# Attention on one core: the maxima's products, and the last scores, issued twice in a row

## The chip, the core and the metric

The kernel runs on one core of a Trainium2 chip. Its time is the device time in microseconds (us); three runs of the kernel before gave 4300.12, 4308.26 and 4286.41, with a median of 4300.12. A core has TensorE (PE, matrix products into the banks of PSUM; its weight loads are shown apart as PEld), VectorE (DVE), ScalarE (ACT), GpSimd (POOL) and SyncE (SP, which issues the transfers). TensorE's clock is granted by the chip: the profile shows it as 1.00 (2.4 GHz) or 0.50 (1.2 GHz), or as a mean of both over a longer stretch.

## What is computed

Two layers follow one another on an input of 2 batches of 1024 tokens of 512 values: attention with 32 heads of 16 values, a gated feed-forward block with low-rank factors, a state-space block ("mamba"), and a second feed-forward block. Each stands between two layer norms and is added to its input. The change touches the attention alone:

```python
q = (x @ Wq.T + bq).reshape(b, l, h, hd).transpose(0, 2, 1, 3)
k = (x @ Wk.T + bk).reshape(b, l, h, hd).transpose(0, 2, 1, 3)
v = (x @ Wv.T + bv).reshape(b, l, h, hd).transpose(0, 2, 1, 3)
scores = jnp.einsum('bhqd,bhkd->bhqk', q, k) / math.sqrt(hd)
scores = jnp.where(causal, scores, -jnp.inf)
att = jax.nn.softmax(scores, axis=-1)
out = jnp.einsum('bhqk,bhkd->bhqd', att, v)
```

## The kernel before

**Tiling.** The batches run one after the other. In a batch the attention goes through eight "quads" of four heads (t = 0 to 7). Queries and keys are split into a high and a low part, and three products of 16 values each stand stacked as one product over 48 rows (`stack_q`, `stack_k`). The scores are wanted twice. First with the queries as rows, 48 products of 48 rows in a quad ("pieces", line 628): VectorE takes the maximum of each row of each product (lines 1237 and 1242), and nothing else is kept of them. The maxima are turned (line 637), split and put by two small transfers into two more rows of `stack_q`. Then the scores with the keys as rows, 48 products of 50 rows in a quad (line 652), which have the maxima subtracted already: ScalarE takes the exponential of two heads at once (line 948) into `probs`, GpSimd zeroes what lies above the diagonal (line 1608), and the products with V (line 671, four heads side by side in the array, each as two instructions) add up in bank 6. These outputs are copied, turned (line 681) and divided into Y.

**Sizes.** Of the twelve pieces of a head six have 512 columns and two each 384, 256 and 128, which is 384 in the mean; the twelve score products of a head have the same sizes.

**Order.** `attention_order()` writes out one order, `ORDER`, that all engines follow. Before quad 0's scores come the first projections, V and quad 0's pieces, with six pieces of quad 1. From then on quad t's scores are mixed with quad t+1's pieces: in each of the twelve steps of a quad four score products, each with a piece or two behind it, then the product with V of the step before. In quads 1 and 3 four projections are mixed in as well (48 products of 128 rows and 512 columns, lines 492 to 494). Quad 7 has no pieces beside it.

**Waits.** The pieces, projections and turns go round three banks (4, 5, 7). A piece waits for `ring_free`, which says that VectorE has read the bank three places before; it raises `ring_done`, for which VectorE waits. The scores use banks 0 to 3: the first of each pair waits for `exp_done` of the step before, the second raises `st_done`, for which ScalarE waits.

Of the kernel before, what the change touches and what calls it, by code (L numbers as in the profile page):

```python
# [24 lines left out]
P = 128  # L25
TT = L // P
KT = D // P
HALF = 512
# [6 lines left out]
NQ = AH // QUAD  # L35
VW = HD + 1
ROWS = 3 * HD
# [26 lines left out]
def build(nc, x, w_attn, qk_bias, bv, bo, w_ffn0, lr0, lr0_const, w_ffn1,  # L64
          w_mamba, w_dt, conv_par, dt_bias, a_log, d_skip, out):
    ctx = ExitStack()
    with ctx:
        def sb(name, shape, dt=F32, stack=ctx):
            return stack.enter_context(nc.sbuf_tensor(name, shape, dt))
# [5 lines left out]
        bank = [banks[:, i, :] for i in range(8)]  # L75
# [26 lines left out]
        with ExitStack() as s:  # L102
            V = sb("V", [P, TT, AH, VW], stack=s)
            with ExitStack() as s2:
                stack_q = [sb("stack_q0", [P, QUAD, L], F32R, stack=s2)]
                stack_k = [sb("stack_k0", [P, QUAD, L], F32R, stack=s2)]
# [380 lines left out]
        def _(pe):  # L487
            pe.wait_ge(consts_ready, 1)

            def three(dst, a_hi, a_lo, w_hi, w_lo, kt, first, last):  # L490

                pe.matmul(dst, a_hi(kt), w_hi(kt), start=first, stop=False)  # L492
                pe.matmul(dst, a_lo(kt), w_hi(kt), start=False, stop=False)  # L493
                return pe.matmul(dst, a_hi(kt), w_lo(kt), start=False, stop=last)  # L494

            def tokens(dst, i, w_hi, w_lo, cols=None):

                tok = slice(i * P, (i + 1) * P)
                for kt in range(KT):
                    r = three(dst, lambda k: xhi[:, k, tok], lambda k: xlo[:, k, tok],  # L500
                              lambda k: w_hi[:, k, :], lambda k: w_lo[:, k, :], kt, kt == 0, kt == KT - 1)
                return r

            def features(dst, w_hi, w_lo, s):

                tok = slice(s * HALF, (s + 1) * HALF)
                for kt in range(KT):
                    r = three(dst, lambda k: w_hi[:, k * P:(k + 1) * P], lambda k: w_lo[:, k * P:(k + 1) * P],
                              lambda k: xhi[:, k, tok], lambda k: xlo[:, k, tok], kt, kt == 0, kt == KT - 1)
                return r  # L510
# [85 lines left out]
            with pe.Fori(0, B) as b:  # L596
# [5 lines left out]
                for what, *arg in ORDER:  # L602
                    if what == "proj":
                        f, use = arg
                        which = use // 2
                        if use == 0:
                            pe.wait_ge(wqk_ready, b * 8 + 2 * f + 2)
                        if ring >= 3:
                            pe.wait_ge(ring_free, b * RING + ring - 2)
                        features(bank[RING_BANKS[ring % 3]][:], wqk_hi[:, which, :], wqk_lo[:, which, :], use % 2  # L610
                                 ).then_inc(ring_done, 1)
                        ring += 1
                    elif what == "values_in":
                        i, = arg
                        if i == 0:
                            pe.wait_ge(wv_ready, b + 1)
                        pe.wait_ge(ring_free, b * RING + ring - 2)
                        tokens(bank[RING_BANKS[ring % 3]][:], i, wv_hi, wv_lo).then_inc(ring_done, 1)
                        ring += 1
                    elif what == "piece":  # L620
                        t, n = arg
                        h, i, s, cols, _ = PIECES[n]
                        base, buf = 64 * (t % 2), t // 2 % 2
                        if n == 0:
                            pe.wait_ge(stacked[t % 2], (b * (NQ // 2) + t // 2 + 1) * STACKED)
                        pe.wait_ge(ring_free, b * RING + ring - 2)
                        dst = bank[RING_BANKS[ring % 3]]
                        r = pe.matmul(dst[:, 0:cols], stack_q[buf][base:base + ROWS, h, i * P:(i + 1) * P],  # L628
                                      stack_k[buf][base:base + ROWS, h, s * HALF:s * HALF + cols],
                                      start=True, stop=True)  # L630
                        r.then_inc(ring_done, 1)
                        ring += 1
                    elif what == "maxima":
                        t, = arg
                        pe.wait_ge(mx_ready, b * NQ + t + 1)
                        pe.wait_ge(ring_free, b * RING + ring - 2)
                        pe.transpose(bank[RING_BANKS[ring % 3]][0:QUAD * TT, 0:P], mx[:, 0, :], ident[:]
                                     ).then_inc(ring_done, 1)
                        ring += 1
                    elif what == "score":  # L640
                        t, n, h = arg
                        s, j = STEPS[n]
                        lo = max(j * P - s * HALF, 0)
                        base, buf = 64 * (t % 2), t // 2 % 2
                        it = b * (NQ * NS) + (t * NS + n)
                        if n == 0 and h == 0 and t % 2 == 0 and t < 4:
                            pe.wait_ge(ones_rows, b * (16 * 8) + 16 * 4 * (t // 2 + 1))
                        if n == 0 and h == 0:
                            pe.wait_ge(mt_in, START + (b * NQ + t + 1) * 32)
                        if h % 2 == 0:  # L650
                            pe.wait_ge(exp_done[h // 2], START + it)
                        r = pe.matmul(bank[h][:, 0:HALF - lo],  # L652
                                      stack_k[buf][base:base + ROWS + 2, h, j * P:(j + 1) * P],
                                      stack_q[buf][base:base + ROWS + 2, h, s * HALF + lo:(s + 1) * HALF],
                                      start=True, stop=True)
                        if h % 2:
                            r.then_inc(st_done[h // 2], 1)
                    elif what == "values":
                        t, n = arg
                        s, j = STEPS[n]  # L660
                        lo = max(j * P - s * HALF, 0)
                        it = b * (NQ * NS) + (t * NS + n)
                        if j == 0:
                            pe.wait_ge(ot_ready, START + b * (2 * NQ) + 2 * t + s)
                        for p in range(2):
                            if j * P >= s * HALF:
                                pe.wait_ge(masked[p], b * (NQ * TT) + (t * TT + j + 1))
                            else:
                                pe.wait_ge(exp_done[p], START + it + 1)
                        for h in range(QUAD):  # L670
                            r = pe.matmul(bank[6][32 * h:32 * h + VW, lo:HALF], V[:, j, QUAD * t + h, :],  # L671
                                          probs[n % 2][:, h, 0:HALF - lo], start=j == 0,
                                          stop=j == CPH * (s + 1) - 1, skip_group_check=True,
                                          tile_position=(0, 32 * h))
                        r.then_inc(pv_done, 1)
                    elif what == "turn":
                        t, s = arg
                        pe.wait_ge(ot_ready, START + b * (2 * NQ) + 2 * t + s + 1)
                        pe.wait_ge(ring_free, b * RING + ring - 2)
                        for k in range(CPH):  # L680
                            r = pe.transpose(bank[RING_BANKS[ring % 3]][:, k * P:(k + 1) * P], ot[:, k * P:(k + 1) * P], ident[:])
                        r.then_inc(ring_done, 1)
                        ring += 1
# [3 lines left out]
                for i in range(TT + 1):  # L687
                    if i < TT:
                        if i >= 2:
                            pe.wait_ge(at_free, b * TT + i - 1)  # L690
                        for k in range(KT):
                            r = pe.transpose(bank[2 + i % 2][:, k * P:(k + 1) * P], Y[:, i, k * P:(k + 1) * P],
                                             ident[:])
# [17 lines left out]
                for s in range(2):  # L711
                    tok = slice(s * HALF, (s + 1) * HALF)
                    for kt in range(KT):
                        r = three(bank[5 + s][0:MH, :], lambda k: wdt_hi[:, k, :], lambda k: wdt_lo[:, k, :],
                                  lambda k: xhi[:, k, tok], lambda k: xlo[:, k, tok], kt, kt == 0, kt == KT - 1)
# [1072 lines left out]
```

## Time and profile before

| | |
|---|---|
| median of three runs | 4300.12 us |
| the profiled execution | 4294.83 us |
| its span, first to last instruction | 4293.1 us |
| mean granted clock of TensorE | 0.907 |
| attention of batch 0 (29 to 478 us) | 449 us at a clock of 0.76 |
| attention of batch 1 (2178 to 2640 us) | 462 us at 0.77 |
| PE busy, share of the span | 90% |

The profile lists what each engine did and when. PE's busy time counts a product from its start to its modelled end, so products that overlap in the pipeline make it look fuller than its columns would. The distance from one start to the next in a dense stream is what a product costs.

### The profile page before, as it was taken

To read this page: it belongs to the slowest core of one execution; us is meant where nothing else is said; L and a number is where in the kernel's file an instruction comes from. 1 tells how busy PE (TensorE), PEld (TensorE's weight loads), DVE (VectorE), ACT (ScalarE), POOL (GpSimd) and SP (SyncE) were. 2 spreads that over 40 slices of the span, in tenths; PEclk is the share of its full clock that TensorE was granted. 3 is DMA by queue.
4 is the path that set the end of the run, shared out by engine and by line. 5 is a ranking of instruction groups with operands and counts; after the bars stand their busy time and mean duration, and the time that the engine had idled before them with its cause. 6 is when DMAs were issued, how large, how long until landed. Compare 5 with 4: busy or idle time off the path is not lost.

```text
span 4293.1 us, 61464 instructions
## 1 busy us (share of the span) xinstructions
PE 3861.4 (90%) x18056; PEld 2813.5 (66%) x18056; DVE 2711.2 (63%) x5034; ACT 1695.2 (39%) x3538; POOL 1880.8 (44%) x2017
## 2 busy tenths in 40 slices
PE   7899799689999999979878896996899999999797
PEld 4444478567777777757654444885677777777576
DVE  3567445577777777764435673555777777777644
ACT  1344411355545555541113444113555555555411
POOL 1111344355555655654311113443555556655542
PEclk8677899899999999989977767998999999999899
DMA  3221011011100111001032210110101001110010
GB/s 73 36 36 31 24 51 45 22 33 30 32 20 25 34 32 29 22 15 45 35 81 36 36 32 29 46 45 22 35 28 32 20 25 34 32 29 22 15 52 35
DMA packets 81456, 145.59 MB, mean 34 GB/s; under 512 B 16392, under 2 KB 18520, under 8 KB 81264
## 3 DMA queue, kind: packets, MB, share of 16 engines
q1 hardware_dynamic: 81264, 143.28, 12.9%
q8 instruction: 90, 1.47, 0.1%
q14 instruction: 102, 0.84, 0.1%
HBM read 113.08 MB, written 4.19 MB: 27 GB/s over the span
## 4 chain that ended last, share of the span: by engine, by line
PE 69%; issue 11%; DVE 7%; ACT 4%; POOL 3%; DVEq 2%; POOLq 2%; DMA 1%; SPq 1%; ACTq 0%
PE banks L492 15%; PE banks L493 14%; PE banks L494 14%; PE banks L832 4%; PE banks L671 4%; PE banks L652 3%; PE banks L628 3%; PE banks L825 2%; PE banks L845 2%; DVE conv L1344 2%; DVEq L1347 1%; PE banks L767 1%; PE banks L768 1%; POOL X L1509 1%; ACT conv L1005 1%
## 5 line engine op out<-in xcount | busy, mean ns | idle before, releaser
L1344 DVE SCALAR_TENSOR_TENSOR conv<-banks,cpar,conv 128x509 f32<-128x509 f32 (+2 forms) x576 | 428.2, 744 | 115.3 <-ACT conv L1005 100.9
L948 ACT ACTIVATE probs<-banks 128x1024 f32<-128x1024 f32 (+3 forms) x384 | 297.7, 810 | 309.4 <-PE banks L652 308.9
L1172 DVE TENSOR_TENSOR Y<-banks,Y 128x512 f32<-128x512 f32 x400 | 276.1, 691 | 188.1 <-PE banks L494 187.9
L1608 POOL TENSOR_SCALAR_AFFINE_SELECT probs<-probs 128x256 f32<-128x256 f32 x256 | 104.2, 408 | 645.8 <-ACT probs L948 645.5
L628 PE MATMUL banks<-stack_k,stack_q 48*128 48x512 f32 (+3 forms) x768 | 331.7, 502 | 59.3 <-DVEq L1218 19.8
L1672 POOL TENSOR_TENSOR state<-state,gt 128x512 f32<-128x512 f32 x112 | 133.5, 1192 | 500.4 <-PE banks L825 500.4
L492 PE MATMUL banks<-xhi,f_hi 128*128 128x512 f32 x800 | 322.6, 403 | 3.5 <-DVE xlo L1143 3.5
L492 PE MATMUL banks<-xhi,wx_hi 128*128 128x512 f32 x768 | 312.0, 406 | 14.4 <-DVE conv L1344 14.4
L493 PE MATMUL banks<-xhi,f_lo 128*128 128x512 f32 x800 | 319.9, 400 | 0.0
L494 PE MATMUL banks<-xlo,f_hi 128*128 128x512 f32 x800 | 319.4, 399 | 0.0
L494 PE MATMUL banks<-xlo,wx_hi 128*128 128x512 f32 x768 | 306.0, 398 | 0.0
L493 PE MATMUL banks<-xhi,wx_lo 128*128 128x512 f32 x768 | 306.0, 398 | 0.0
L1237 DVE CUSTOM_DVE_ANT_0 banks<-banks,mask_qk 128x128 f32<-128x128 f32 (+3 forms) x512 | 248.1, 500 | 72.7 <-PE banks L628 59.4
L832 PEld LDWEIGHTS banks<-xdt,decay 128*128 128x128 f32 x2048 | 248.5, 192 | 65.2 <-issue 65.2
L652 PE MATMUL banks<-stack_q,stack_k 50*128 50x512 f32 (+3 forms) x768 | 274.7, 459 | 5.2 <-ACT probs L948 2.9
L628 PEld LDWEIGHTS banks<-stack_k,stack_q 48*128 48x128 f32 x768 | 163.0, 235 | 157.9 <-DVE mx L1242 51.1
L492 PE MATMUL banks<-wg_hi,xhi 128*128 128x512 f32 x512 | 222.3, 434 | 45.5 <-DVE conv L1344 42.2
L652 PEld LDWEIGHTS banks<-stack_q,stack_k 50*128 50x128 f32 x768 | 157.0, 232 | 155.5 <-issue 116.8
L832 PE MATMUL banks<-xdt,decay 128*128 128x64 f32 x2048 | 242.7, 272 | 2.4 <-DVE decay L1363 2.4
L910 ACT CAST h_hi<-hf 128x512 fp32r<-128x512 f32 x100 | 62.2, 622 | 441.0 <-DVE hf L1161 441.0
L518 PE MATMUL banks<-ident,xn 128*128 128x128 f32 x256 | 66.5, 426 | 188.1 <-ACT xn L892 165.3
L1076 ACT ACTIVATE yv<-banks,gt 128x64 f32<-128x64 f32 x1024 | 223.8, 332 | 24.8 <-PE banks L825 24.8
(209 smaller groups left out, 10185.0 us busy)
## 6 DMA issues: line engine op xcount, KB each, us to landing
m_raw<-in_w_mamba SPq DMA_DIRECT2D x224, 256.0 KB, 2.6
f_raw<-in_w_ffn SPq DMA_DIRECT2D x50, 768.0 KB, 4.5
stack_q<-part_hi SPq DMA_DIRECT2D x128, 64.0 KB, 2.4
stack_k<-part_hi SPq DMA_DIRECT2D x128, 64.0 KB, 2.5
X<-in_x SPq DMA_DIRECT2D x4, 1024.0 KB, 6.5
wqk_raw<-in_w_attn SPq DMA_DIRECT2D x8, 512.0 KB, 3.5
stack_q<-part_lo SPq DMA_DIRECT2D x64, 64.0 KB, 2.4
stack_k<-part_lo SPq DMA_DIRECT2D x64, 64.0 KB, 2.5
```

Source lines behind the costliest of these rows:

```text
L492: pe.matmul(dst, a_hi(kt), w_hi(kt), start=first, stop=False)
L493: pe.matmul(dst, a_lo(kt), w_hi(kt), start=False, stop=False)
L494: return pe.matmul(dst, a_hi(kt), w_lo(kt), start=False, stop=last)
L628: r = pe.matmul(dst[:, 0:cols], stack_q[buf][base:base + ROWS, h, i * P:(i + 1) * P], stack_k[buf][base:base + ROWS, h, s * HALF:s * HALF ...
L652: r = pe.matmul(bank[h][:, 0:HALF - lo], stack_k[buf][base:base + ROWS + 2, h, j * P:(j + 1) * P], stack_q[buf][base:base + ROWS + 2, h, s ...
L671: r = pe.matmul(bank[6][32 * h:32 * h + VW, lo:HALF], V[:, j, QUAD * t + h, :], probs[n % 2][:, h, 0:HALF - lo], start=j == 0, stop=j == C ...
L832: r = pe.matmul(bank[7][:, h * MP:(h + 1) * MP], decay[:, h, :], xdt[:, h * MP:(h + 1) * MP], start=True, stop=True, skip_group_check=True)
L948: act.activation(probs[n % 2][:, 2 * p:2 * p + 2, 0:w], banks[:, 2 * p:2 * p + 2, 0:w], ACT.Exp, scale=1.0 / HD ** 0.5).then_inc(exp_done[ ...
L1076: r = act.activation(yv[:, own], bank[6][:, own], ACT.Identity, scale=gt[:, EC, c, h:h + 1])
L1172: dve.tensor_tensor(Y[:, i, :], bank[6 + i % 2], Y[:, i, :], ALU.add).then_inc(f["dn_used"], 1)
L1237: dve.tensor_tensor_reduce(out=src, in0=src, in1=mask_qk[:, HALF - cols:HALF], scale=1.0, scalar=NEG, op0=ALU.add, op1=ALU.max, accum_out= ...
L1344: r = dve.scalar_tensor_tensor(out=rest, in0=src[:, 0:HALF - lag], scalar=cpar[:, o:o + 1], in1=rest, op0=ALU.mult, op1=ALU.add)
```

## The change

The product for the maxima is issued once for quad 0 and twice for quads 1 to 7, both times with the same operands into the same columns of the same bank; the waits stand ahead of the first, and `ring_done` is raised by the second. The score products of quad 7 are issued twice in the same way, and `st_done` is raised by the second of the pair's second head. All results stay the same, and no other engine's program changes. Each product loads its weights itself, so a weight load is added with each.

```diff
@@ piece
                         dst = bank[RING_BANKS[ring % 3]]
-                        r = pe.matmul(dst[:, 0:cols], stack_q[buf][base:base + ROWS, h, i * P:(i + 1) * P],
-                                      stack_k[buf][base:base + ROWS, h, s * HALF:s * HALF + cols],
-                                      start=True, stop=True)
+                        for _ in range(1 if t == 0 else 2):
+                            r = pe.matmul(dst[:, 0:cols], stack_q[buf][base:base + ROWS, h, i * P:(i + 1) * P],
+                                          stack_k[buf][base:base + ROWS, h, s * HALF:s * HALF + cols],
+                                          start=True, stop=True)
                         r.then_inc(ring_done, 1)
@@ score
                             pe.wait_ge(exp_done[h // 2], START + it)
-                        r = pe.matmul(bank[h][:, 0:HALF - lo],
-                                      stack_k[buf][base:base + ROWS + 2, h, j * P:(j + 1) * P],
-                                      stack_q[buf][base:base + ROWS + 2, h, s * HALF + lo:(s + 1) * HALF],
-                                      start=True, stop=True)
+                        for _ in range(2 if t == NQ - 1 else 1):
+                            r = pe.matmul(bank[h][:, 0:HALF - lo],
+                                          stack_k[buf][base:base + ROWS + 2, h, j * P:(j + 1) * P],
+                                          stack_q[buf][base:base + ROWS + 2, h, s * HALF + lo:(s + 1) * HALF],
+                                          start=True, stop=True)
                         if h % 2:
                             r.then_inc(st_done[h // 2], 1)
```

## Rows read from the trace of the kernel before

**Rows 1.** The page's slices: busy tenths of PE, and the granted clock.
```profile
PE   7899799689999999979878896996899999999797
PEclk8677899899999999989977767998999999999899
```
**Rows 2.** Busy time by stretch: both attentions, their parts with pieces, their last quads.
```profile
core 0: us, PE busy (x) PEld busy (x) DVE busy (x) ACT busy (x) POOL busy (x), PEclk, DMA share, GB/s
29.00:478.00 449.00, 406.23 (x1903) 206.18 (x1904) 245.40 (x738) 159.67 (x209) 70.35 (x137) 0.76 0.20 36
2178.00:2640.00 462.00, 418.67 (x1981) 218.38 (x1981) 253.01 (x748) 163.78 (x215) 68.73 (x136) 0.77 0.20 35
...
123.00:446.00 323.00, 300.72 (x1488) 140.82 (x1492) 204.69 (x631) 135.69 (x176) 51.64 (x114) 0.72 0.20 34
2272.00:2590.00 318.00, 294.71 (x1500) 138.16 (x1499) 203.14 (x623) 137.78 (x178) 52.80 (x117) 0.74 0.22 37
```
**Rows 3.** The stretches at low clock between 123 and 437 us, all instructions: thirteen stretches.
```profile
123.00:157.50 34.50, 33.40 (x135) 15.40 (x137) 22.42 (x73) 13.28 (x16) 3.27 (x8) 0.50 0.61 103
...
369.10:396.40 27.30, 27.19 (x117) 11.38 (x115) 16.86 (x54) 10.54 (x14) 2.45 (x6) 0.50 0.00 1
410.10:437.40 27.30, 27.23 (x118) 11.61 (x117) 17.11 (x54) 10.95 (x14) 2.74 (x7) 0.50 0.00 1
sum 181.20, PE 177.15 PEld 80.43 DVE 104.67 ACT 62.34 POOL 21.67; mean PE 13.63 PEld 6.19 DVE 8.05 ACT 4.80 POOL 1.67
```
**Rows 4.** The stretches at high clock between 157 and 446 us: thirteen stretches.
```profile
352.00:369.10 17.10, 16.00 (x110) 7.61 (x106) 13.64 (x44) 9.97 (x13) 4.08 (x10) 1.00 0.25 43
396.40:410.10 13.70, 12.60 (x86) 6.12 (x86) 11.40 (x36) 7.64 (x11) 3.80 (x10) 1.00 0.02 5
...
sum 141.80, PE 123.58 PEld 60.39 DVE 100.03 ACT 73.35 POOL 29.97; mean PE 9.51 PEld 4.65 DVE 7.69 ACT 5.64 POOL 2.31
```
**Rows 5.** Batch 1's twelve stretches at low clock, 2270 to 2574 us: all instructions, their sum.
```profile
sum 167.10, PE 163.31 PEld 75.03 DVE 100.46 ACT 56.33 POOL 23.48; mean PE 13.61 PEld 6.25 DVE 8.37 ACT 4.69 POOL 1.96
```
**Rows 6.** Line 628 alone in the low-clock stretches of batch 0 (170 in all).
```profile
123.00:157.50 34.50, 20.75 (x41) 10.88 (x42) 0.50 0.61 103
...
369.10:396.40 27.30, 14.25 (x28) 7.05 (x27) 0.50 0.00 1
410.10:437.40 27.30, 14.59 (x28) 7.29 (x28) 0.50 0.00 1
```
**Rows 7.** The same in the low-clock stretches of batch 1 (159 in all).
```profile
2270.30:2297.60 27.30, 17.55 (x34) 8.86 (x33) 0.50 0.63 106
...
2546.80:2574.10 27.30, 16.02 (x31) 8.02 (x31) 0.50 0.01 2
```
**Rows 8.** Timeline at low clock (start, length): products of 512 columns in a dense stream.
```profile
178.10 0.63 PE L492 MATMUL banks<-xhi,wqk_hi 128*128 128x512 f32 x1
178.53 0.63 PE L493 MATMUL banks<-xhi,wqk_lo 128*128 128x512 f32 x1
178.95 0.63 PE L494 MATMUL banks<-xlo,wqk_hi 128*128 128x512 f32 x1
```
**Rows 9.** Stretches of 20 us in the attention and in the feed-forward block.
```profile
240.00:260.00 20.00, 20.00 (x91) 9.36 (x93) 13.05 (x41) 9.07 (x11) 0.50 (x2) 0.50 0.61 99
...
2700.00:2720.00 20.00, 20.00 (x91) 16.30 (x91) 9.63 (x14) 3.04 (x5) 11.98 (x13) 1.00 0.13 41
```
**Rows 10.** The page on line 628: all of both batches, and what PE's idle time before it waited for.
```profile
L628 PE MATMUL banks<-stack_k,stack_q 48*128 48x512 f32 (+3 forms) x768 | 331.7, 502 | 59.3 <-DVEq L1218 19.8
```
**Rows 11.** Line 628 from 123 to 446 us: PE's idle time before it, by releaser.
```profile
L628 PE MATMUL banks<-stack_k,stack_q x336: 217/496/794, 123.5 to 441.7; 48*128 48x512 f32 x112, 48*128 48x128 f32 x28, 48*128 48x384 f32 x28
its engine sat idle before it (us, times) until:
  DVE mx L1242: 27.4, 71
  DVE mx L1237: 18.9, 45
  DVEq L1218: 16.0, 16
```
**Rows 12.** The last 3.4 us at high clock ahead of a fall, and the last quad.
```profile
454.40:478.00 23.60, 20.28 (x143) 8.91 (x143) 3.17 (x7) 14.75 (x21) 11.28 (x14) 1.00 0.00 1
...
365.70:369.10 3.40, 3.12 (x19) 1.70 (x15) 3.22 (x10) 2.62 (x3) 0.82 (x2) 1.00 0.01 2
```
**Rows 13.** Groups of instructions from 446 to 478 us, quad 7 of batch 0.
```profile
L948 ACT ACTIVATE probs<-banks 128x1024 f32<-128x1024 f32 (+3 forms) x25 | 18.5, 792 | 9.1 <-PE banks L652 9.1
L652 PE MATMUL banks<-stack_q,stack_k 50*128 50x512 f32 (+3 forms) x48 | 13.1, 381 | 1.7 <-ACT probs L948 1.5 <-DMA stack_q<-mt_lo 0.2
```
**Rows 14.** The timeline from 365.7 to 368.2 us on PE and ACT, ahead of the same fall.
```profile
365.73 0.49 PE L652 MATMUL banks<-stack_q,stack_k 50*128 50x512 f32 x1
...
365.73 0.50 PE L628 MATMUL banks<-stack_k,stack_q 48*128 48x512 f32 x1
...
367.56 0.44 PE L652 MATMUL banks<-stack_q,stack_k 50*128 50x384 f32 x1
...
368.14 0.50 PE L628 MATMUL banks<-stack_k,stack_q 48*128 48x512 f32 x1
```

## The prediction

> **What bounds the kernel now.** I read the page's slices first: PE is busy nearly everywhere, but the granted clock is below 1.00 mostly in the slices of the two attentions [rows 1]. Then busy time by stretch: the attentions last 449 and 462 us with a mean clock of 0.76 and 0.77, while VectorE is busy 245 of the 449 and ScalarE 160 [rows 2]. So TensorE sets the pace, at a clock that changes. I therefore cut the part in which pieces and scores are mixed (123 to 446 us, and 2272 to 2590) at every change of the clock, and asked for each kind of stretch by itself. At low clock PE is busy 177 of 181 us in batch 0 and 163 of 167 in batch 1 [rows 3, 5]: whatever is added there is paid in full. At high clock it is busy 124 of 142 us and VectorE 100 [rows 4]; a typical one, 396.4 to 410.1, has VectorE at 11.4 of 13.7. There the two engines run close together, and PE waits for VectorE to free a bank: before line 628 it sat idle 27.4 and 18.9 us for the two kinds of maximum and 16.0 us for the drain behind a projection, out of 323 us [rows 11]. The reader is to see that the mixed part has two regimes of about equal work, one with no slack on PE and one with some.
>
> **How many, and at what price.** The change adds products and their weight loads on TensorE, moves nothing, removes nothing, and touches no queue and no transfer. Pieces of quads 1 to 7: 7 x 48 x 2 batches = 672 of 48 rows. Scores of quad 7: 48 x 2 = 96 of 50 rows. A product of 512 columns costs 0.427 us at low clock, from start to start in a dense stream [rows 8], and 20.00 / 92 = 0.217 us at high clock (91 to 92 in 20 us, [rows 9]). The mean piece has 384 columns, three quarters of it: 0.320 and 0.163 us. The rows of price are of 128-row products; for 48 rows there is no dense stream in the trace to read it from, but 117 and 118 products fill 27.3 us at low clock wholly [rows 3], so I take the same price and no surcharge. The weight load lies beside the product ahead of it: it is busy 11.4 of the 27.3 us in which the products are busy all the time [rows 3]. For the smallest pieces (128 columns, two of twelve) the load might not be hidden; even at 0.1 us for each of those 112, an estimate as large as half the 0.213 us that 256 columns take at low clock, it would be 11 us, and I leave it to the range.
>
> **The pieces at low clock.** Of line 628's products 170 lie in low-clock stretches in batch 0 and 159 in batch 1 [rows 6, 7]; a second issue of each costs 329 x 0.320 = 105 us. PE's idle time there is 4 + 4 us in all, so I count it whole: +105. What it delays is everything behind it in PE's queue: the next score, for which ScalarE waits, and the next product with V. VectorE, which waits for `ring_done`, starts each maximum 0.32 us later, with 105 of 181 us busy it has room.
>
> **The pieces at high clock.** The other 672 - 329 = 343 cost 343 x 0.163 = 56 us of PE. Here PE has slack, but it isn't free for them: the second issue stands behind the same wait as the first, so it can hide only by running while the other two banks of the ring still hold work for VectorE. Bounds: 0 (all in the gaps) and 56 (all on the path). In the stretch 396.4 to 410.1 PE is busy 12.6 of 13.7 us, whose 21 pieces would add 3.4 us; VectorE needs 11.4. Neither covers it all. I take half, +28.
>
> **The scores of quad 7.** 96 x 0.163 = 15.6 us. ScalarE is busy 18.5 of 32 us there and idle 9.1 us waiting for these very products [rows 13]; each pair's exponential starts two products later than before. Bounds 0 and 16; PE is not full (20.3 of 23.6 us, [rows 12]) but most of the chain goes through it. I take two thirds, +10.
>
> **The clock.** The sum so far holds the clock of each stretch as it was. What does the doubled work do to it? The trace shows when it falls. From 365.7 to 369.1 PE is busy 3.12 of 3.40 us, almost only with products of 48 and 50 rows [rows 12, 14], and behind it the clock is 0.50 for 27.3 us [rows 3]. Quad 7 has no pieces, PE is emptier (20.28 of 23.60), and it keeps 1.00 all through [rows 12]. And 240 to 260 us has PE busy 20.00 of 20.00 at 0.50 the whole time, where the feed-forward block with as full a PE runs at 1.00 [rows 9]. So products of 48 rows, even dense, have not held the clock in this kernel; the products over 128 rows (V, projections) do. Doubling the pieces makes the mix poorer in those. I take no gain and no loss of clock for the forecast.
>
> The Trainium skill ("TensorE: Matmul & The Clock Gate", Part 1, and its table of goals) says that the clock follows how busy the PE has been, and advises to keep it busy without gaps; by that the filler products would raise it. The rows on 240 to 260 us and 365.7 to 369.1 us disagree with busy time alone as the measure; what that rule would give here is rival A.
>
> **Sum.** 105 + 28 + 10 = +143 us on the profiled execution's 4294.8 us: 4438 us. The profiled execution lies 5 us under the median of the runs shown, so against the median it is +3.2%.
>
> **Rivals.**
>
> A, the clock stays up (faster). The second issue fills the gaps of the high-clock stretches, above all at the border of two quads where the clock falls now, and the low stretches vanish. Price: the 181 + 167 = 348 us at low clock would be bounded by VectorE, busy 104.7 + 100.5 = 205 us there [rows 3, 5]; in a high stretch it is 11.4 of 13.7, or 0.83, so they would last 205 / 0.83 = 247 us, 101 less. All 672 pieces are then issued at 0.163, 110 us, of which half on the path, 55, and quad 7's 10: -36, so 4259 us. It decides at the border of quads: if the clock is still 1.00 there, nothing later pulls it down. For it: the gap to a full PE is small there, and the trace has no stretch of 48-row products without any gap at high clock. Against it: PE was already busy 3.12 of 3.40 and the clock fell.
>
> B, part of it. Some of the falls are avoided, those that come where products with V stand among the pieces, others not. Halfway between the forecast and A: 4349 us.
>
> C, the clock falls more. The high stretches end earlier since 128-row products lie further apart. A high stretch does 86 products in 13.7 us and a low one 117 in 27.3 [rows 3, 4], 6.3 against 4.3 per us, so each us of high clock that turns low costs 0.47 us. If a quarter of the 142 + 154 us at high clock turns, that is 74 x 0.47 = 35 us and some 10 us more because the added pieces there lose their cover: 4438 + 45 = 4483 us.
>
> D, hidden or without effect: the second issue costs nothing since another wait ends last. It would need slack where PE is busy 177 of 181 us; about 4300 to 4320.
>
> **Chances.** Forecast 0.50, A 0.13, B 0.17, C 0.14, D 0.06. About 0.5% (21 us) is what a measurement of this kernel can tell from no change. Faster by over 0.5%: A, 0.13. Within 0.5%: most of D and the lower edge of B, 0.08. Slower: the rest, 0.79. The forecast's own bounds are 105 + 0 + 0 and 105 + 56 + 16 + 11, so 4400 to 4483. For 8 in 10 I reach up to C (4495) and down through most of B (4330), which leaves out A, D and the far end of C.
>
> **What would show it.** Right: 768 more products on PE, line 628 with 1440 instead of 768 [rows 10]; the mixed parts some 65 us longer each, with a mean clock near the 0.72 and 0.74 of before; low-clock stretches of a quad without projections some 36 instead of 27 us; quad 7 about 5 us longer; all else unchanged. Wrong: a clock of 1.00 across the border of quads, with VectorE at over 0.8 of the mixed part (A); high stretches shorter than 13.7 us in quads 5 and 6 (C). If pieces at high clock turn out wholly hidden, 28 us go; if a score in quad 7 is hidden too, 10 more.

## The result, and the profile after

The changed kernel took 4346.44 us (median of four runs, 4335.71 to 4355.68) against 4299.14 for the kernel before on the same chip: a ratio of 1.010, 95% interval 1.008 to 1.013. It is slower, as forecast, but by 47 us and not by 143. The profiled execution has a span of 4353.9 us, 60.8 more than the one before; it is the slowest of the four runs, 9 us above their median.

The page of the changed kernel: the two slices of [rows 1], the counts of [rows 10], and ScalarE's group. Its lines below 628 have moved down by one or two: 629 are the pieces, 654 the scores, 673 the products with V.

```profile
PE   7999889789999999979779998897899999999797
PEclk8797889899999999989977987898999999999899
...
L629 PE MATMUL banks<-stack_k,stack_q 48*128 48x512 f32 (+3 forms) x1440 | 432.4, 431 | 46.3 <-DVEq L1220 17.4
L950 ACT ACTIVATE probs<-banks 128x1024 f32<-128x1024 f32 (+3 forms) x384 | 303.4, 810 | 359.6 <-PE banks L654 358.8
```

The 1440 pieces are there, 672 more. What answers to [rows 2] is the busy time of the same two stretches and of both attentions (start and end, length, then busy us of PE, PEld, DVE, ACT and POOL, the granted clock, and DMA):

```profile
29.00:503.00 474.00, 439.73 (x2281) 259.37 (x2282) 252.84 (x737) 162.50 (x208) 70.16 (x137) 0.80 0.20 34
2200.00:2678.00 478.00, 443.37 (x2282) 257.63 (x2283) 250.62 (x737) 162.80 (x208) 69.72 (x137) 0.79 0.19 34
...
123.00:446.00 323.00, 305.78 (x1725) 174.39 (x1724) 205.19 (x612) 129.00 (x164) 49.02 (x108) 0.79 0.21 34
2272.00:2590.00 318.00, 296.24 (x1626) 168.33 (x1625) 196.35 (x585) 121.13 (x154) 45.00 (x99) 0.81 0.21 35
```

The part in which pieces and scores are mixed runs at a *higher* clock than before, 0.79 and 0.81 for 0.72 and 0.74. That is against the forecast. What happened is seen quad by quad. I took the turn of the maxima (one small transpose on PE for each quad) as the border of the quads. First the kernel before, quads 2, 5 and 6 of batch 0:

```profile
224.30:265.60 41.30, 39.75 (x202) 18.09 (x201) 28.60 (x89) 18.59 (x25) 6.53 (x16) 0.67 0.54 91
361.20:402.60 41.40, 40.14 (x201) 17.55 (x201) 28.55 (x89) 18.62 (x25) 6.53 (x16) 0.67 0.01 2
402.60:443.70 41.10, 39.89 (x201) 17.73 (x201) 28.51 (x89) 18.61 (x25) 6.53 (x16) 0.67 0.01 2
```

and its quad 7 in both batches:

```profile
443.70:477.20 33.50, 28.28 (x187) 12.02 (x188) 4.68 (x11) 19.82 (x28) 14.50 (x22) 0.95 0.12 41
...
2583.60:2617.50 33.90, 28.80 (x188) 12.48 (x188) 4.68 (x11) 19.78 (x28) 14.49 (x22) 0.91 0.13 41
```

Then the changed kernel: quads 2, 5, 6 and 7 of batch 0, and 2, 4, 5, 6 and 7 of batch 1:

```profile
234.40:270.50 36.10, 34.93 (x251) 18.57 (x250) 28.67 (x89) 18.75 (x24) 6.50 (x16) 1.00 0.62 102
...
366.70:414.50 47.80, 47.44 (x250) 27.57 (x250) 30.42 (x89) 19.11 (x24) 6.50 (x16) 0.64 0.01 2
414.50:462.40 47.90, 47.55 (x251) 27.79 (x250) 30.53 (x89) 19.12 (x24) 6.51 (x16) 0.64 0.01 2
462.40:502.80 40.40, 37.08 (x236) 20.91 (x236) 4.68 (x11) 20.46 (x28) 14.56 (x22) 0.90 0.11 34
...
2405.70:2441.80 36.10, 34.94 (x250) 18.59 (x250) 28.66 (x89) 18.76 (x25) 6.50 (x16) 1.00 0.60 101
...
2501.60:2537.40 35.80, 34.64 (x250) 18.44 (x249) 28.46 (x89) 18.72 (x25) 6.50 (x16) 1.00 0.55 90
2537.40:2586.80 49.40, 49.05 (x250) 27.92 (x249) 30.47 (x89) 19.12 (x25) 6.51 (x16) 0.62 0.01 2
2586.80:2622.60 35.80, 34.64 (x250) 18.45 (x249) 28.48 (x89) 18.73 (x25) 6.50 (x16) 1.00 0.01 3
2622.60:2677.70 55.10, 52.21 (x236) 27.68 (x236) 4.68 (x11) 21.07 (x28) 14.52 (x22) 0.61 0.07 25
```

The reader is to see two kinds of quad in the place of one among quads 2 and 4 to 6, which have no projections. Before, each was a mixture, 38 to 41 us at a clock of 0.67 to 0.78. After, four of the eight are wholly at high clock and *shorter* than before, 36 us, with 48 more products in them (a fifth, quad 4 of batch 0, nearly so: 37.2 us at 0.95), and in three the clock fell for long and they take 48 to 49. Quad 7 went from 33.5 and 33.9 to 40.4 and 55.1 us. Added up, quads 0 to 6 of both batches cost 24 us more in these two traces (half of it in quad 0), quad 7 costs 28, and the part ahead of quad 0, which the change doesn't touch, 7 (98.1 and 98.0 us against 94.1 and 94.7, at a clock of 0.79 and 0.76 against 0.84 and 0.81).

### The profile page after: what moved, and what is told of

Its sections match the earlier page's. It is cut to its first block, busy times and chain, and to the rows that moved or that the text cites. A ratio compares the mean times of both kernels' runs of the same rounds, so it can differ in the third digit from the quotient of the medians.

```text
span 4353.9 us, 63000 instructions
## 1 busy us (share of the span) xinstructions
PE 3940.6 (91%) x18824; PEld 2922.9 (67%) x18824; DVE 2724.1 (63%) x5034; ACT 1699.9 (39%) x3538; POOL 1878.1 (43%) x2017
## 4 chain that ended last, share of the span: by engine, by line
PE 71%; issue 11%; DVE 6%; ACT 4%; POOL 3%; POOLq 2%; DVEq 2%; SPq 1%; DMA 1%; ACTq 0%
PE banks L492 15%; PE banks L493 14%; PE banks L494 14%; PE banks L629 6%; PE banks L834 4%; PE banks L673 4%; PE banks L654 4%; PE banks L827 2%; PE banks L847 2%; DVE conv L1346 2%; DVEq L1349 1%; PE banks L769 1%; PE banks L770 1%; POOL X L1511 1%; ACT conv L1007 1%
## 5 line engine op out<-in xcount | busy, mean ns | idle before, releaser
L629 PE MATMUL banks<-stack_k,stack_q 48*128 48x512 f32 (+3 forms) x1440 | 432.4, 431 | 46.3 <-DVEq L1220 17.4
L629 PEld LDWEIGHTS banks<-stack_k,stack_q 48*128 48x128 f32 x1440 | 276.2, 227 | 134.9 <-DVE mx L1244 40.5
L654 PE MATMUL banks<-stack_q,stack_k 50*128 50x512 f32 (+3 forms) x864 | 290.4, 441 | 0.4 <-DMA stack_q<-mt_lo 0.4
L654 PEld LDWEIGHTS banks<-stack_q,stack_k 50*128 50x128 f32 x864 | 171.2, 222 | 131.3 <-issue 114.0
```

The source lines that it names most:

```text
L654: r = pe.matmul(bank[h][:, 0:HALF - lo], stack_k[buf][base:base + ROWS + 2, h, j * P:(j + 1) * P], stack_q[buf][base:base + ROWS + 2, h, s ...
```

## The experiments

Each run's median is set against the kernel before on the same chip, with the ratio and its 95% interval in brackets. The medians of before are 4301.38 us for the first four runs, 4310.65 for the next four and 4301.29 for the last four. The theories: **R**, the clock follows how much of the array's rows the products fill, so fillers (added products whose results nobody uses) over more rows hold it better; **B**, PE's busy time alone sets it; **pure cost**, the prediction's sum with no effect on the clock.

**One part alone: the pieces twice, quad 7's scores once.**

```diff
-                        for _ in range(2 if t == NQ - 1 else 1):
-                            r = pe.matmul(bank[h][:, 0:HALF - lo],
+                        r = pe.matmul(bank[h][:, 0:HALF - lo],
```

> The products for the maxima twice, the scores of quad 7 once. In the changed kernel quad 7 took 40.4 us in batch 0 and 55.1 in batch 1, against 33.5 and 33.9 before, so 28 of its 59 us more in the span came from the doubled scores. Theory R (the clock follows how much of the array's rows the products fill; doubled 48-row products hold it if it is high and can't bring it back if it is low): the rest remains, 4346 - 28 = 4318 us, with some quads near 36 us wholly at high clock and some near 48 us mostly at low clock. Theory B (busy time alone sets the clock): the same time, 4318, so it is the fillers below that part R and B. Rival C of pure cost (the prediction's sum, no effect on the clock): 4300 + 133 = 4433 us.

Measured: 4342.28 us (ratio 1.008, 1.005 to 1.011; ten runs from 4313.9 to 4351.9, the last of them the traced one). Pure cost, 4433, is out, and so is the 4318 of R and B: the 28 us of quad 7 did not come back. Quad 6 and quad 7 of batch 0:

```profile
422.10:458.10 36.00, 34.84 (x251) 18.58 (x250) 28.60 (x90) 18.74 (x24) 6.52 (x16) 1.00 0.01 3
458.10:504.10 46.00, 42.48 (x189) 17.61 (x188) 4.68 (x11) 20.32 (x28) 14.51 (x22) 0.56 0.08 30
```

Quad 7 has nothing added, has a quad wholly at high clock ahead of it, and yet runs at 0.56 and takes 46 us, where it took 33.5 in the kernel before. So the time of quad 7 changes with what came before, even in code that is unchanged. The clock goes down in it in the kernel before as well, at nearly the same place, but comes back. The stretches at low clock of quad 7 of batch 0, in the kernel before and in this run:

```profile
451.00:454.40 3.40, 3.35 (x15) 1.29 (x15) 0.26 (x1) 0.92 (x2) 0.82 (x2) 0.50 0.18 67
```

```profile
463.60:504.10 40.50, 38.10 (x152) 15.59 (x153) 3.43 (x8) 17.79 (x24) 12.92 (x18) 0.50 0.06 23
```

They begin 7.3 and 5.5 us after the quad does. It is the return of the clock that differs.

**The other part alone: quad 7's scores twice, all else as before.**

```diff
+                        for _ in range(2 if t == NQ - 1 else 1):
+                            r = pe.matmul(bank[h][:, 0:HALF - lo],
```

> The scores of quad 7 twice, everything else as before. Pure cost: 2 x 5 us, 4310. Theory R: quad 7 has only 50-row products and those with V, doubling the first thins out the second, so a quad that falls to low clock can't leave it: between +13 us (both batches at high clock, 40 us each) and +43 us (both at low clock, 55 us each), 4313 to 4343. Theory B: fuller PE holds the clock, +13 at the most.

Measured: 4355.94 us (1.012, 1.007 to 1.017), more than the whole change and outside what I expected. Quad 7 was at low clock in both batches:

```profile
443.00:496.30 53.30, 49.79 (x236) 27.15 (x235) 4.68 (x11) 20.55 (x28) 14.50 (x22) 0.66 0.08 26
2623.00:2683.30 60.30, 57.05 (x237) 30.30 (x236) 4.72 (x12) 21.19 (x28) 14.49 (x22) 0.56 0.07 23
```

That is 20 and 26 us more than before for 48 products each. PE was fuller than before in both (93% and 95%, after 84% and 85%), so busy time alone (B) doesn't hold the clock. Quads 0 to 6 of batch 1, where nothing was added, took 329 us in this trace and 315 in that of before: single traces differ by such amounts in unchanged code.

**Fillers over 128 and over 16 rows.** The first of the two products is replaced by another one of as many columns, whose result the second writes over.

```diff
+                        if t > 0:
+                            pe.matmul(dst[:, 0:cols], xhi[:, h, i * P:(i + 1) * P], xhi[:, h, 0:cols],
+                                      start=True, stop=True)
                         r = pe.matmul(dst[:, 0:cols], stack_q[buf][base:base + ROWS, h, i * P:(i + 1) * P],
```

> As the maxima twice, but the first of the two is a product of the same columns over 128 rows (of the normed input, thrown away: the second one writes over it). Same number of products and columns as in the run with the maxima twice. Theory R: the clock stays at 1.00 in quads 0 to 6, each of the quads without projections takes some 36 us as those at high clock did in the changed kernel (41 before), quads 1 and 3 some 56 (58 to 61 before): 8 x 4.5 + 2 x 4 + 4 x 3 = 56 us less than before, some 4245 us. Theory B: no different from the 48-row filler, 4318. Pure cost: 4433.

The filler of 16 rows takes rows `base` to `base + HD` of `stack_q` and `stack_k`.

> As the maxima twice, but the first of the two is a product over 16 rows alone, same columns, thrown away. Theory R: the clock is low in nearly all of quads 0, 2, 4, 5, 6, which take 48 to 50 us (41 before), and quads 1 and 3 some 65: 10 x 8 + 4 x 5 = 100 us more than before, some 4400 us. Theory B: as with the 48-row filler, 4318.

Measured: 4817.59 us and 4903.95 us (1.120 and 1.140). Neither theory had that, and R's forecast for 128 rows, 4245, failed by the most: the clock stayed down with the widest filler of all, with PE busy throughout. 80 us of the first run:

```profile
305.00:385.00 80.00, 80.00 (x230) 31.45 (x230) 27.97 (x78) 15.91 (x21) 5.28 (x13) 0.50 0.14 24
```

A filler's rows alone don't hold the clock, then. Both runs have a cost of their own, which makes them poor tests of it. The timeline of the first, PE alone, at low clock (start, length):

```profile
300.30 0.79 PE L629 MATMUL banks<-xhi 128*128 128x512 f32 x1
301.02 0.79 PE L631 MATMUL banks<-stack_k,stack_q 48*128 48x512 f32 x1
301.02 0.68 PE L655 MATMUL banks<-stack_q,stack_k 50*128 50x384 f32 x1
301.74 0.79 PE L629 MATMUL banks<-xhi 128*128 128x512 f32 x1
302.47 0.79 PE L631 MATMUL banks<-stack_k,stack_q 48*128 48x512 f32 x1
```

Between products of 128 rows and of 48 the starts are 0.72 us apart, where they are 0.427 in a stream of one kind [rows 8]: 0.29 us at each change. The Trainium skill ("TensorEngine Tiling (Array Packing)", Key Properties) says that changing the tiling mode drains the engine; the starts 0.29 us further apart agree with that. The timeline also shows something else: the piece (line 631) and the score product (655) start at the same time, 301.02. By their operands' partitions (`base = 64 * (t % 2)`, with t one apart) one stands in the lower 64 rows of the array and the other in the upper 64.

**Fillers over 64 and over 34 rows**, both in the same half of the rows as the piece, so that nothing is switched. Same number of products and columns, both from `xhi`; only the rows differ.

```diff
+                        if t > 0:
+                            pe.matmul(dst[:, 0:cols], xhi[base:base + 64, h, i * P:(i + 1) * P],
+                                      xhi[base:base + 64, h, 0:cols], start=True, stop=True)
```

> Each product for the maxima of quads 1 to 7 is preceded by one of the same columns over 64 rows of the normed input, in the same half of the array's rows (the fillers of 128 and of 16 rows changed the number of rows the array is set up for, and PE stood still at each change: this one doesn't). Its result is written over by the second. Theory R (what counts for the clock is the share of the array that works): more quads than with 48 rows twice stay at high clock from end to end (36 us), at least 9 of the 14 mixed ones: 4250 to 4300 us. Theory B (busy time alone): no different from the maxima twice, 4342 us.

> The same with a filler over 34 rows in the same half. Theory R: fewer quads at high clock throughout than with 48 rows twice (there 5 of the 8 without projections and past quad 0), at most 2: 4370 to 4420 us. Theory B: 4342 us as with the maxima twice.

Measured: 4297.74 us with 64 rows (0.998, 0.996 to 1.000) and 4429.58 with 34 (1.026, 1.022 to 1.031); with 48, above, 4342.28. The mean clock of the traced runs goes the same way, 0.924, 0.886 and 0.910. Three sizes, in order, 132 us from end to end with the same number of products and columns, and the runs of the three don't overlap: B is out, and R holds for fillers that leave the array's setting as it is. Its counts were off all the same. With 64 rows seven quads of the traced run are at 1.00 from end to end, where it asked for nine; with 48 there are six, with 34 none, and 4430 us lies above its 4370 to 4420. The 48-row fillers repeat the piece's own operands and ran on another chip, so the strict comparison is 64 against 34 rows. More rows also mean more values of `xhi` in the array; whether the data count beside the rows was not tested. With 64 rows, quads 5, 6 and 7 of batch 0 and quad 3 of batch 1:

```profile
365.90:403.80 37.90, 36.62 (x251) 19.25 (x250) 28.68 (x89) 18.81 (x24) 6.54 (x16) 0.95 0.01 2
403.80:439.70 35.90, 34.74 (x251) 18.56 (x250) 28.48 (x89) 18.75 (x24) 6.54 (x16) 1.00 0.01 3
439.70:485.10 45.40, 41.52 (x189) 17.20 (x188) 4.68 (x11) 20.22 (x28) 14.52 (x22) 0.58 0.09 30
2418.30:2473.40 55.10, 47.95 (x299) 27.20 (x298) 31.55 (x93) 21.83 (x28) 9.90 (x18) 1.00 0.03 6
```

With 34 rows, quads 5 and 6 of batch 0:

```profile
389.80:437.60 47.80, 47.45 (x250) 27.52 (x249) 30.36 (x89) 19.11 (x24) 6.50 (x16) 0.64 0.01 2
437.60:485.50 47.90, 47.55 (x250) 27.61 (x249) 30.51 (x89) 19.13 (x24) 6.50 (x16) 0.64 0.01 2
```

A quad at 1.00 takes 36 us with fillers of 64 as of 48 rows, and one at 0.64 takes 48 with 34 as with 48 rows: the rows change how long the clock is down, and not the price of the filler.

**Where the fillers must stand: the first 14 of a quad's 48, or the other 34.**

```diff
+                        for _ in range(2 if t > 0 and n < 14 else 1):
```

> Only the first 14 of a quad's 48 products for the maxima are issued twice, those that come in the last two steps of the quad before and the first two of its own, where the clock falls in the kernel before. Theory G (the gain is made at the border of quads, the price is paid by all fillers in low-clock stretches): a high clock survives the border as often as with all twice, and a quad at low clock costs 14/48 of the surcharge, 2.5 instead of 8 us: below 4300, some 4275 us. Rival H (the filler must be everywhere, since the clock falls inside the quad as well): 14/48 of the prediction's price of 133 us without a gain, 4340 us.

The other run has `n >= 14`.

> The complement: the other 34 of the 48 twice, none at the border. Theory G: the clock falls at the border as before, each of the 14 mixed quads has its low stretch, and 34/48 of the price is paid: 4300 + 94 = 4394 us, no quad of 36 us. Rival H: some quads stay high, about 4342 us.

Measured: 4321.98 us (1.002, 1.000 to 1.005) and 4351.19 (1.009, 1.006 to 1.012). Neither G nor H as I put them. With the border alone no quad was at 1.00 from end to end, though two came to 36.4 and 36.7 us; with the inside alone two took 36.3 us, with the clock down for 3.4 of them. So both places count. But these runs give the price of an added product at an unchanged mean clock. The border's fillers, quads 2 and 4, then the inside's, quad 5, all at 0.67:

```profile
226.40:268.30 41.90, 40.91 (x215) 20.23 (x215) 29.15 (x89) 18.74 (x25) 6.50 (x16) 0.67 0.52 90
329.20:371.00 41.80, 40.81 (x216) 20.24 (x216) 29.01 (x89) 18.74 (x25) 6.50 (x16) 0.67 0.48 77
```

```profile
367.00:413.00 46.00, 45.36 (x235) 24.30 (x234) 30.06 (x89) 18.75 (x24) 6.50 (x16) 0.67 0.01 2
```

The kernel before has 41.1 to 41.4 us at 0.67. The first 14 added products cost 0.5 us together, the other 34 cost 4.6 us: 0.04 and 0.14 us each.

**Fillers of 64 rows in quad 7 as well**, in all its twelve steps, or in the first four:

```diff
+                        if t == NQ - 1:
+                            pe.matmul(bank[h][:, 0:HALF - lo], xhi[base:base + 64, h, j * P:(j + 1) * P],
+                                      xhi[base:base + 64, h, s * HALF + lo:(s + 1) * HALF], start=True, stop=True)
```

> The fillers of 64 rows ahead of each product for the maxima of quads 1 to 7, as before in this study (4298 us), and one ahead of each of quad 7's 48 score products. Theory R: quad 7, which ran at low clock for 38 and 41 of its 45 and 46 us, keeps the high clock and takes 40 us, as the one with doubled scores at high clock did in the changed kernel: 2 x 5.5 us less, 4287. Theory B: PE is fuller, the same. If the fall comes from the wait for the transfers at the start of quad 7, where PE has nothing to do, fillers don't help and the quad takes 55 us: 4318.

> The same, but quad 7's fillers only in its first four steps of twelve, where the clock falls. Theory R: the quad keeps the high clock and then costs little more than the 33.5 us of the kernel before, some 35: 2 x 11 us less than 4298, 4276 us, below the kernel before (4300).

Measured: 4305.45 us (1.001, 0.999 to 1.003; twelve runs from 4278.4 to 4330.4) and 4302.60 (1.000, 0.998 to 1.002). With all twelve steps the traced run, 4283.4 us of span, has quad 7 as expected in both batches, where the clock goes down as before but comes back after 3.4 us. With the first four steps it fell all the same:

```profile
430.60:470.40 39.80, 36.38 (x237) 19.84 (x235) 4.68 (x11) 20.45 (x28) 14.56 (x22) 0.94 0.11 35
2571.00:2610.30 39.30, 35.80 (x235) 19.59 (x235) 4.68 (x11) 20.22 (x28) 14.56 (x22) 0.94 0.10 35
```

```profile
431.90:480.80 48.90, 45.81 (x206) 20.93 (x205) 4.70 (x12) 20.44 (x28) 14.53 (x22) 0.57 0.09 28
```

The forecasts of 4287 and 4276 us failed. The median of the first stays above its traced run by over 20 us; that quad 7 or others fall in many of its executions is likely, but a single trace can't say it.

**Fillers of 64 rows at the border and in quad 7's first four steps alone.**

```diff
-                        if t > 0:
+                        if t > 0 and n < 14:
```

> 64-row fillers only ahead of the first 14 products of each quad's 48 and in quad 7's first four steps. Theory R with the price at the fillers: the border holds the clock more often than with 48 rows there (4322), and the inside of a quad pays nothing: some 4270 us. If the inside needs them as well (the run with the inside alone twice kept two quads nearly all at high clock), it falls between: 4300.

Measured: 4313.41 us (1.002, 1.000 to 1.003), neither 4270 nor 4300. No gain; quads 2 and 4 to 6 come to 36.5 to 39.3 us at clocks below 1.00, but quad 7 takes 44.6 in both batches.

**The price by itself: the pieces three times.**

```diff
-                        for _ in range(1 if t == 0 else 2):
+                        for _ in range(1 if t == 0 else 3):
```

> Each product for the maxima three times, all over 48 rows. It measures the price of an added product by itself. If it is that of a stream of its own (the prediction's 0.320 us at low clock and 0.163 at high), a quad wholly at high clock goes from 36 to 44 us and one mostly at low clock from 49 to 64: 4342 + 14 x 11 = 4500 us. If an added product runs beside the score products in the other half of the rows, as the start times of the changed kernel suggest, half of it is hidden: 4342 + 14 x 5.5 = 4420 us.

Measured: 4456.38 us (1.035, 1.030 to 1.040), 114 us over two times, midway between the two prices. Quad 5 of batch 0, wholly at high clock, and quad 5 of batch 1, mostly at low:

```profile
401.20:442.50 41.30, 41.03 (x299) 26.32 (x298) 30.48 (x89) 19.25 (x24) 6.53 (x16) 1.00 0.01 3
...
2600.60:2659.10 58.50, 58.23 (x299) 36.05 (x298) 31.13 (x89) 19.47 (x24) 6.53 (x16) 0.67 0.01 2
```

At high clock the third product costs (41.3 - 36.0) / 48 = 0.11 us, and in a quad mostly at low clock (58.5 - 49.4) / 48 = 0.19 us, though at a mean clock of 0.67 where the quad with two had 0.62.

## Why the prediction was wrong in size

**What bounds the kernel: half right.** TensorE at a clock that changes, yes. "At low clock ... whatever is added there is paid in full" is the first step that failed. PE's modelled busy time, 177 of 181 us, was read as an array without slack. The array is two halves here: pieces of quad t+1 stand in one half of the rows and scores of quad t in the other, and they stream side by side. The trace of before shows it in the very rows that I quoted: at 365.73 us a score product and a piece start together [rows 14]. In the changed kernel at low clock (start, length; `x3` is three products in a row):

```profile
390.77 0.79 PE L654 MATMUL banks<-stack_q,stack_k 50*128 50x512 f32 x1
390.77 1.01 PE L629 MATMUL banks<-stack_k,stack_q 48*128 48x128 f32 x3
391.36 0.62 PE L654 MATMUL banks<-stack_q,stack_k 50*128 50x512 f32 x1
391.58 0.41 PE L629 MATMUL banks<-stack_k,stack_q 48*128 48x256 f32 x1
391.79 0.62 PE L654 MATMUL banks<-stack_q,stack_k 50*128 50x512 f32 x1
```

From the second on, the score products follow each other 0.43 us apart, the step of a dense stream at low clock, with the doubled small pieces wholly beside them. A second issue costs little as long as it runs beside a product of the other half; the third costs more, 0.11 us at high clock, with PE busy 41.0 of 41.3 us. The Trainium skill says that tiles of the array operate independently ("TensorEngine Tiling (Array Packing)", Key Properties), and the starts at 390.77 agree.

**The price: the low-clock term was mis-sized, by about three.** The terms were 0.320 us a piece at low clock (+105 us) and half of 0.163 at high (+28). At a clock of 0.67, 34 added products should have cost some 8 us, taking two thirds of them at low clock; they cost 4.6. For all 48, 14 + 34 together, that is 5.1 us a quad, so over 14 quads some 70 us where I had 133. This is worked out from quads without projections; that quads 1 and 3 pay the same was not measured.

The two kinds of quad give an estimate by another way. Before, a quad took 38.0 us with 17.1 at low clock (quad 4 of batch 0) and 41.1 with 27.3 (quad 6), so each us at low clock adds 0.30 and a quad wholly at high clock would take some 33. With 48 more it took 36.0 with none at low clock and 47.8 with 34.1, which is 0.35 for each. The 48 then cost some 3 us at high clock, or 0.07 each, close to the half of 0.163 that I took; and at the old 27.3 us of low clock some 4.4, of which 28 pieces at low clock pay some 3, or 0.11 each in the place of 0.320.

**The clock: the step that turned out wrong in kind.** "I take no gain and no loss of clock" and "products of 48 rows, even dense, have not held the clock". They do, when they are doubled: four quads of the traced run hold 1.00 from end to end, and six in the run with the pieces alone, in each of which it fell before. By the mean clocks of quads 0 to 6, 0.72 and 0.73 before, 0.79 and 0.83 after, the time at low clock went from some 350 to some 250 us. At 0.3 us each that is a gain of about 30 us, which with 14 x 4.4 = 62 us of price leaves some 30, near the 24 in the traces. The evidence that I drew on, 3.12 of 3.40 us busy ahead of the fall, was again modelled busy time.

The rival A was the right mechanism in the quads that hold (36 us, VectorE busy 28.7 of them, 0.79, near the 0.83 I used), and its point, the border of the quads, was one of two places. C, high stretches that end earlier, is not what happened in those that fell. Quads 5 and 6 of batch 0, in which the clock changes three times:

```profile
371.90:406.00 34.10, 34.10 (x155) 20.78 (x152) 20.38 (x57) 12.40 (x15) 3.25 (x8) 0.50 0.01 1
406.00:419.70 13.70, 13.35 (x100) 6.84 (x97) 10.05 (x32) 6.71 (x10) 3.25 (x8) 1.00 0.02 5
419.70:453.80 34.10, 34.10 (x159) 20.80 (x152) 20.47 (x57) 12.29 (x15) 3.26 (x8) 0.50 0.00 1
```

The high stretch is the 13.7 us of before, and the low ones are 34.1 for 27.3, close to the "some 36" of the forecast. So the forecast's picture came true in the three quads that fell and A's in those that hold. That is B, "part of it": 4349 us for 4346 measured. The number of B is partly luck, as it was a mere halfway value with quad 7 at +10; but that some quads would hold and others fall is what the trace shows.

**Quad 7: term mis-sized.** +10 us forecast, +28 in the trace, and +46 with its scores doubled alone. Mostly at high clock it costs 6.5 to 7 us a batch, not far from the 5 of the forecast (33.5 and 33.9 to 40.4). The rest is the fall: mostly at low clock it takes 55 us. I had said that quad 7 "keeps 1.00 all through". That was a wrong reading: the row from 454.4 to 478 us begins where the low stretch of 451.0 to 454.4, shown above, ends.

**The start of each attention**, 7 us in the trace, is in no part of the prediction. Its code is unchanged, and in batch 0 nothing that was changed has run before it. Among the traced runs it took 94.1 to 98.4 us in batch 0, so these 4 us at least are a difference between executions.

In the two traces, then, quads 0 to 6 cost 24 us where the sum had 133, quad 7 costs 28 where it had 10, and 7 lie ahead of them where it had nothing.

**A slip in the sum.** The +143 us were added to the profiled 4294.8 and then compared with the median of 4300.12: against that it would be 4443 us, or 3.3%.

**What stays open.** Why the clock comes back after 3.4 us in quad 7 of the kernel before, in both batches, and stays down for 24 to 40 us in all ten unchanged quads 7 of the five traced runs with the pieces doubled (all, border or inside) or preceded by fillers of 34 or 64 rows; and whether 64-row fillers through all of quad 7 could be made to hold in every execution, in which case the kernel would take some 4285 us, as its traced run did, and not 4305.

## What to carry to other kernels

Before pricing an added product, look at which rows of the array it stands in and what streams in the others: modelled busy time says nothing about that, the start times do. Where, as here, a part of a kernel flips between the clock's two levels, price a change once at either level and ask which way it tips each stretch, since the two can cancel: here 36 against 48 us around an old 41. Of the work that was added here to hold the clock, only the fillers that fill a half of the rows without changing the array's setting paid for themselves, and even they came back to the time of the kernel before and no further. A stretch cut out of a trace at a change of the clock hides the change: look at what lies just ahead of it.

## What the runs showed of the hardware

- With the same number of products and columns, fillers over 34, 48 and 64 rows gave 4430, 4342 and 4298 us, at a mean clock of 0.886, 0.910 and 0.924. Fillers over 128 rows, each with a change of the array's setting around it, gave 0.855; in 80 us of it PE is busy all the time at 0.50.
- A change between products of 128 and of 48 rows costs 0.29 us at low clock; 672 fillers with a change on either side added 516 us, and those of 16 rows among products of 48 added 603.
- Products over 48 rows in one half of the array's rows and 50 in the other start at the same time and stream side by side.
- Unchanged code (quad 7) took 33.5 us at a clock of 0.95 and 46 us at 0.56.
